# Two softmaxes of a decoder layer: sums taken before the turn, weights turned after the exponentials

## What is computed

```python
# self attention, 16 heads of 8
scores = einsum('bhid,bhjd->bhij', Q, K) / sqrt(8) + einsum('bhid,ijd->bhij', Q, rel_table[rel_idx])
ctx = einsum('bhij,bhjd->bhid', softmax(scores), V);  out = ctx @ Wo + bo
# cross attention, 16 heads of 64, keys and values from the 77 context tokens
sim = einsum('bihd,bjhd->bhij', x @ Wq, context @ Wk) * 64**-0.5
out = einsum('bhij,bjhd->bihd', softmax(sim), context @ Wv) @ Wo
```

## Time and profile before

| | |
|---|---|
| runs | 845.19, 846.94, 856.15 us; median 846.94 |
| profiled execution | 846.87 us, its span 845.1 us |
| busy, share of the span | TensorE 718.3 us (85%), VectorE 518.2 (61%), ScalarE 417.1 (49%), GpSimd 205.9 (24%) |
| mean granted TensorE clock | 0.938 of full speed |

### The profile page before, as it was taken

How to read it: one execution, slowest core, us unless ns; L and a number is a source line. 1 busy time by engine, 2 the same in 40 slices (tenths; PEclk the granted TensorE clock), 3 DMA queues, 4 the chain that set the end, 5 groups by cost and what they waited for, 6 DMA issues and landing times. The chain is left out here.

```text
span 845.1 us, 22574 instructions
## 1 busy us (share of the span) xinstructions
PE 718.3 (85%) x9462; PEld 538.8 (64%) x9462; DVE 518.2 (61%) x1447; ACT 417.1 (49%) x1188; POOL 205.9 (24%) x212
## 2 busy tenths in 40 slices
PE   5788998999998798999874887898888888988873
PEld 3466776677776576776664685666666666766641
DVE  1343665555557655655565575777878877788732
ACT  3745656456556355566432122345555554555531
POOL 5210011111101110115314022334333334333200
PEclk9989999999999799999998796999999999999975
DMA  9534444233444214444422110000000000110000
GB/s 361 206 123 129 153 154 154 104 126 93 141 154 154 107 48 154 153 151 153 144 90 101 50 41 17 8 11 15 14 12 11 12 11 13 15 16 11 5 5 6
DMA packets 48261, 72.30 MB, mean 86 GB/s; under 512 B 2832, under 2 KB 43280, under 8 KB 45472
## 3 DMA queue, kind: packets, MB, share of 16 engines
q1 hardware_dynamic: 45120, 61.80, 21.5%
q0 software_dynamic: 2320, 5.18, 2.8%
q10 hardware_dynamic: 720, 3.88, 1.2%
HBM read 32.38 MB, written 38.47 MB: 84 GB/s over the span
## 5 line engine op out<-in xcount | busy, mean ns | idle before, releaser
L403 POOL TENSOR_TENSOR rext<-rext,ones 128x1008 f32<-128x1008 f32 x16 | 29.9, 1867 | 320.5 <-ACT rext L919 320.5
L934 ACT ACTIVATE sc<-sc,nmxa 128x128 f32<-128x128 f32 x256 | 78.2, 388 | 7.0 <-DVE nmxa L1149 6.3
L972 ACT ACTIVATE pTb<-bank 77x512 f32<-77x512 f32 x128 | 66.8, 590 | 7.3 <-PE bank L486 7.3
L1199 DVE TENSOR_REDUCE nmb<-bank 128x4 f32<-128x308 f32 x128 | 53.7, 472 | 16.6 <-PE bank L486 16.5
L1438 DVE TENSOR_TENSOR k<-bank,k_sb 128x512 f32<-128x512 f32 x64 | 41.2, 685 | 35.5 <-PE bank L486 35.5
L1145 DVE TENSOR_TENSOR sc<-bank,rel 128x512 f32<-128x512 f32 x64 | 41.1, 684 | 21.3 <-PE bank L486 21.3
L464 POOL TENSOR_SCALAR k<-k 128x256 f32<-128x256 f32 x16 | 13.8, 860 | 160.2 <-ACT k L1048 160.2
L486 PE MATMUL bank<-k,xdT 128*128 128x512 f32 x96 | 49.3, 654 | 0.0
L919 ACT ACTIVATE rext<-bank 128x512 f32<-128x512 f32 x64 | 35.6, 592 | 27.0 <-PE bank L486 27.0
L534 PE MATMUL bank<-k_sb,sc 128*128 128x128 f32 x256 | 42.3, 289 | 7.0 <-ACT sc L934 4.7
L486 PE MATMUL bank<-nmT,k_sb 32*77 32x128 f32 x1024 | 47.6, 280 | 0.0
(11 more groups left out here) (267 smaller groups left out, 1744.5 us busy)
## 6 DMA issues: line engine op xcount, KB each, us to landing
rel_dram<-rext SPq DMA_DIRECT2D x16, 2040.0 KB
rel<-rel_dram SPq DMA_DIRECT2D x16, 960.0 KB, 5.5
rext<-w_up SPq DMA_DIRECT2D x1, 1792.0 KB, 10.7
rel<-w_down SPq DMA_DIRECT2D x1, 1792.0 KB, 7.7
wb<-w_b ACTq DMA_DIRECT2D x1, 1604.0 KB, 16.5
xT_ld<-xT SPq DMA_DIRECT2D x16, 64.0 KB, 6.8
x_all<-x ACTq DMA_DIRECT2D x1, 1024.0 KB, 11.7
rel<-rel_dram SPq DMA_DIRECT2D x16, 64.0 KB, 5.8
```

What stands on the lines that cost most here:

```text
L403: G.tensor_tensor(rext[:, :, 0:MAX_REL - 1], rext[:, :, MAX_REL - 1:MAX_REL].broadcast_to(shape), ones[:, 0:1].unsqueeze(2).broadcast_to(s ...
L934: last = A.activation(sc[:, h, :], sc[:, h, :], ACT.Exp, bias=nmxa[:, h:h + 1])
L972: A.activation(dst[0:C, 4 * i:4 * i + 4, :], bank[b][0:C, :].rearrange("p (a i) -> p a i", a=4), ACT.Exp).then_inc(exped["b"], 1)
L1199: V.tensor_reduce(nmb[:, 32 * i:32 * i + 4], bank[b][:, 0:4 * C].rearrange("p (a j) -> p a j", a=4), AX.X, ALU.max, negate=True).then_inc( ...
```

## The change

The cross attention's scores stay with the queries on the partitions. VectorE subtracts the maxima while it copies them from the banks to `pB` in SBUF (`b_l0` to `b_l3`), ScalarE takes the exponentials there, four of 128x308; the banks are free from `b_l` on, and `v0`, `b_v`, `b_r` and others use them meanwhile. VectorE sums 8 heads at a time (`b_sum0`, `b_sum1`) and takes reciprocals (`b_rec0`, `b_rec1`), GpSimd multiplies `pB` by them (`b_n0`, `b_n1`, 128x616 each), TensorE turns the 16 heads by transposes (`b_t0` to `b_t3`), and ScalarE and VectorE copy two banks each to `pTb`. `b_u0`, `b_u1` become plain copies. `b_nm`, `b_st0`, `b_st1`, `b_inj`, `b_sm0`, `b_sm1` and `b_rc` are gone.

In the self attention each of the 16 exponentials also writes the sum of its row (`accum_out`). VectorE takes the reciprocals (`a_rec`), widens them to 128x128 (`a_rw`), TensorE transposes this (`a_rT`) and ScalarE copies it to `rba`; the sums by matmul and the Ln and Exp are gone.

`ORDER1` is new for all engines but SP, with a deeper pipeline: `a_s` of a sequence is in round t, `b_t` and `b_out` in t+3, the logits in t+4, the slots in t+5. `r_send` handles one sequence a round instead of a batch. `pB` lies over the key weights, `x1` has three buffers, and some semaphores of loop 2 are replaced by others that exist already.

```diff
 ORDER1 = {
-    "pe": ("b_inj:-1 a_t2 a_t3 a_qkv:2 a_v b_sm0:-1 b_sm1:-1 b_v0:-1 b_v1:-1 rel_last:2 a_out b_out:-1 rel:2 "
-            "v0 b_r:-1 b_x b_lg:-1 r_rank:-2 a_s:1 b_q b_s0 b_s1 a_t0:1 b_st0 b_nm a_t1:1 b_st1").split(),
+    "pe": ("b_t0:-3 b_t1:-3 b_t2:-3 b_t3:-3 a_s b_q:-2 b_s0:-2 a_v:-1 a_qkv:2 b_s1:-2 a_rT:-1 b_v0:-3 b_v1:-3 "
+            "a_out:-1 b_r:-4 b_out:-3 rel_last:2 b_lg:-4 v0:-2 r_rank:-5 rel:2 b_x:-1 a_t0 a_t1 a_t2 a_t3").split(),
+    "dve": ("b_norm:-4 b_t1:-3 b_t3:-3 a_m0 a_m1 b_qhi:-2 b_m0:-2 b_m1:-2 b_l0:-2 b_m2:-2 b_l1:-2 b_l2:-2 "
+            "b_m3:-2 a_div:-1 b_l3:-2 b_u0:-3 b_u1:-3 a_qkv:2 a_add:-1 b_sum0:-2 a_st:-1 rel_last:2 a_ag:-1 "
+            "b_sum1:-2 b_rec0:-2 b_add:-3 b_lg:-4 a_ln:-1 r_a:-4 a_rec b_rec1:-2 b_st:-3 r_b:-4 a_rw r_c:-5 "
+            "b_ag:-3 a_t1 v0:-2 a_t3").split(),
+    "act": ("a_t0:-1 b_ln:-4 a_t2:-1 b_t0:-3 b_t2:-3 b_qlo:-2 a_e0 a_e1 a_qkv:2 a_rT:-1 b_e0:-2 b_e1:-2 a_e2 "
+            "b_e2:-2 b_r:-4 b_e3:-2 a_e3 a_ln:-1 r_a:-4 v0:-2 rel0:2 rel1:2 rel2:2 rel3:2 b_x:-1").split(),
+    "pool": "r_send:-12 rel_fill:2 b_n0:-1 b_n1:-1".split(),
...
+        early = sb("early", [P, H * C])
+        wk = early[:, 0:WK_N]
+        pB = early[:, :].rearrange("p (h j) -> p h j", j=C)
...
+        x1 = [sb(f"x1{i}", [P, P]) for i in range(3)]
...
+            def b_even_(j):
+                def f(t):
+                    pool.wait_ge(recips["b"], 2 * t + 1 + j)
+                    part = slice(8 * j, 8 * j + 8)
+                    G.tensor_tensor(pB[:, part, :], pB[:, part, :], recb[:, part].unsqueeze(2).broadcast_to([P, 8, C]),
+                                    ALU.mult).then_inc(b_even, 1)
...
             def send(t):
+                pool.wait_ge(r_slots, 2 * sum(1 for b in BATCHES if b[0] <= t) - 1)
...
             def a_scores(t):
                 pe.wait_ge(a_kv, t + 1)
-                need(pe, var["a"], t)
+                need(pe, a_pT_act, 2 * t)
+                need(pe, a_pT_dve, 2 * t)
...
             def a_turn(i):
                 def f(t):
                     pe.wait_ge(exped["a"], 4 * t + i + 1)
+                    if t + 2 < B:
+                        pe.wait_ge(r_mid, 4 * (t + 2) + i + 1)
...
+            def a_rT_(t):
+                pe.wait_ge(recips["a"], t + 1)
...
+                pe.transpose(bank[1][:, P:2 * P], recw[:], ident).then_inc(a_rT_ps, 1)
...
+            def b_turn(i):
+                def f(t):
+                    pe.wait_ge(b_even, 2 * t + 1 + i // 2)
...
+                    for a in range(4):
+                        last = pe.transpose(bank[(6, 7, 4, 5)[i]][0:C, a * P:(a + 1) * P], pB[:, 4 * i + a, :], ident)
+                    last.then_inc(turned, 1)
...
             def b_values(j):
                 def f(t):
-                    pe.wait_ge(exped["b"], 4 * t + 2 + 2 * j)
+                    pe.wait_ge(b_pT_act, 2 * t + 1 + j)
+                    pe.wait_ge(b_pT_dve, 2 * t + 1 + j)
+                    if t + 1 < B:
+                        pe.wait_ge(maxed["b"], 4 * (t + 1) + 1 + 2 * j)
...
             def a_exp(i):
...
-                        last = A.activation(sc[:, h, :], sc[:, h, :], ACT.Exp, bias=nmxa[:, h:h + 1])
+                        last = A.activation(sc[:, h, :], sc[:, h, :], ACT.Exp, bias=nmxa[:, h:h + 1],
+                                            accum_out=suma[:, h:h + 1])
...
+            def b_exp(i):
+                def f(t):
+                    act.wait_ge(maxed["b"], 4 * t + i + 1)
+                    part = pB[:, 4 * i:4 * i + 4, :]
+                    A.activation(part, part, ACT.Exp).then_inc(exped["b"], 1)
...
+            def a_wide(t):
+                past("a_rec", t)
+                need(dve, a_rT_ps, t)
+                V.tensor_copy(recw[:].rearrange("p (h d) -> p h d", d=DH), reca[:].unsqueeze(2).broadcast_to([P, H, DH])
+                              ).then_inc(recips["a"], 1)
...
+            def a_div(t):
+                dve.wait_ge(a_rT, t + 1)
+                dve.wait_ge(values["a"], t + 1)
+                V.tensor_tensor(oTa[:], bank[0][:, 0:P], rba[:], ALU.mult).then_inc(oT_ready["a"], 1)
...
+            def b_less(i):
+                def f(t):
+                    past(f"b_m{i}", t)
+                    need(dve, turned, 4 * (t - 1) + i + 1)
+                    V.tensor_tensor(pB[:, 4 * i:4 * i + 4, :], bank[(6, 7, 4, 5)[i]][:, 0:4 * C].rearrange(
+                        "p (a j) -> p a j", a=4), nmxb[:, 4 * i:4 * i + 4].unsqueeze(2).broadcast_to([P, 4, C]), ALU.add
+                        ).then_inc(maxed["b"], 1)
...
+            def b_sum(j):
+                def f(t):
+                    dve.wait_ge(exped["b"], 4 * t + 2 + 2 * j)
+                    keep(f"b_sum{j}", t, V.tensor_reduce(sumb[:, 8 * j:8 * j + 8], pB[:, 8 * j:8 * j + 8, :], AX.X, ALU.add))
```

More of the change, by code:

```diff
@@ L700, in _ @@
                 "a_qkv": a_qkv_, "rel": rel_scores, "rel_last": rel_last,
-                "a_s": a_scores, **{f"a_t{i}": a_turn(i) for i in range(4)}, "a_v": a_values, "a_out": a_out,
-                "b_x": b_x, "b_q": b_q_, "b_s0": b_scores(0), "b_s1": b_scores(1), "b_nm": b_nm, "b_st0": b_turn(0),
-                "b_st1": b_turn(1), "b_inj": b_inj, "b_sm0": b_sums_(0), "b_sm1": b_sums_(1),
+                "a_s": a_scores, **{f"a_t{i}": a_turn(i) for i in range(4)}, "a_v": a_values, "a_rT": a_rT_, "a_out": a_out,
+                "b_x": b_x, "b_q": b_q_, "b_s0": b_scores(0), "b_s1": b_scores(1), **{f"b_t{i}": b_turn(i) for i in range(4)},
                 "b_v0": b_values(0), "b_v1": b_values(1), "b_out": b_out,
@@ L1212, in b_mul, with b_out, f @@
+            def b_out(j):
+                def f(t):
+                    dve.wait_ge(values["b"], 2 * t + j + 1)
+                    V.tensor_copy(oTb[:, 4 * j:4 * j + 4, :], bank[4 if j else 6][:].rearrange(
+                        "p (c i) -> p c i", c=4)).then_inc(oT_ready["b"], 1)
                 return f
@@ L1327, in _ @@
                 "a_qkv": a_kv_, "rel_last": rel_last, "a_m0": a_max(0), "a_m1": a_max(1), "a_t1": a_turn(1),
-                "a_t3": a_turn(3), "a_div": divide("a", 0, rba[:], oTa[:]),
-                "a_add": add("a", 1, lambda t: x_all[:, t, :]), "a_st": stats_("a"), "a_ag": moments("a"), "a_ln": norm("a", lambda t: x1[t % 2][:], normed["a"]),
-                "b_qhi": b_qhi_, **{f"b_m{i}": row_max(i, (6, 7, 4, 5)[i]) for i in range(4)},
-                "b_u0": b_mul(0), "b_u1": b_mul(1), "b_add": add("b", 7, lambda t: x1[t % 2][:]),
+                "a_t3": a_turn(3), "a_rec": a_recips, "a_rw": a_wide, "a_div": a_div,
+                "a_add": add("a", 1, lambda t: x_all[:, t, :]), "a_st": stats_("a"), "a_ag": moments("a"), "a_ln": a_norm,
+                "b_qhi": b_qhi_, **{f"b_m{i}": b_max(i) for i in range(4)},
+                **{f"b_l{i}": b_less(i) for i in range(4)},
+                "b_t1": b_turn(1), "b_t3": b_turn(3), "b_sum0": b_sum(0), "b_sum1": b_sum(1), "b_rec0": b_recips(0), "b_rec1": b_recips(1),
+                "b_u0": b_out(0), "b_u1": b_out(1), "b_add": add("b", 7, lambda t: x1[t % 3][:]),
                 "b_st": stats_("b"), "b_ag": moments("b"),
```

216 lines of the change are left out of this document (122 added, 94 removed).

## The result

The changed kernel takes 823.83 us (median of 819.17 to 825.33) against 847.16 for before: ratio of the means 0.9695, 95% interval 0.9616 to 0.9774. The forecast was 823. The time is right, but not all of its steps are: the steady round came out 2 us shorter than was forecast, and the start and the routing batches cost most of that back.

What follows compares the result with a forecast made beforehand. It took TensorE's own instructions to bound loop 1's round before. A walked round of 21.75 plus 0.3 and 0.45 gave 22.5; loop 1 ending at 446 against 469.9 saved 24 us: 845.1 - 24 + 1.8 = 823, range 806 to 850.

Steps and rivals of the forecast that it cites:

- The forecast's own case: Loop 1's steady round becomes 22.0 to 23.1 us, the time 817 to 832; chance 0.45.
- rival A: Accumulators and GpSimd holds both cost nothing in loop 1: round 21.3 to 21.8, time 806 to 814; chance 0.15.
- The path: Loop 1's new round walked from b_t0 over VectorE, TensorE and ScalarE in turn: 21.75 us before two additions.
- The charge of 0.3 for accumulators: ScalarE's accumulator sums in the self attention delay the round by 0.3 us, at 0.2 us extra per exponential.
- x: Extra price of accum_out per ScalarE exponential in the self attention: taken as 0.2 us, bounds 0 to 0.305.
- The charge of 0.45 for holds: GpSimd's fill and b_n0 hold VectorE's b_norm and a_ln, adding 0.45 us a round.
- Batch 0, 8 us: Routing batch 0's VectorE chains in loop 1, pick 6 and slots 2.5, cost 8 us, against 11.4 before.
- Rounds 0 to 2: Loop 1's first rounds, chains without full cross attention, take 17, 14 and 16.5 us; round 3 starts at 81.5.
- TensorE's floor of 20.5: TensorE's work per round of loop 1 falls from 22.7 to 20.5 us, the floor of the new round.
- D: ScalarE becomes the bound at 0.5 us extra per exponential: round 25.5 or more, time 862 and up; chance 0.11.
- C: Round gains nothing, VectorE held longer or accumulators dearer: round 23.2 to 24.5, time 833 to 850; chance 0.29.
- TensorE's own instructions set the round: In loop 1 of before, TensorE is busy 22.7 of the steady round's 23.86 us and so bounds it.

Runs made afterwards that it cites:

- e7: The changed kernel with each b_sum done twice on VectorE, the first result unused; 826.7 us, steady round 20.91.
- e8: The changed kernel with one more unused 128x512 reduction in a_m1 on VectorE, ahead of b_qhi; 848.7 us, round 23.93 in the trace.
- e11: e8 with the 32 unused matmul records of the self attention's sums added on TensorE behind a_v; 833.6 us, round 21.27.
- e3: The changed kernel without accum_out on the self attention's 16 exponentials, row sums a constant 8; 823.0 us, round 20.55.
- e1: The changed kernel with rel_fill ahead of the two sends in GpSimd's queue; 821.2 us, round 20.55.
- e6: e1 with VectorE's two normalisations, b_norm and a_ln, moved out of GpSimd's instructions; 821.2 us, round 20.81.
- e5: The kernel before with only the self attention's half of the change; 845.7 us against 849.9 for before, round 24.12.
- e9: e6 with the pick of a batch moved on VectorE one round later, behind b_u1; 807.3 us, ratio 0.9481 to before.
- e13: The changed kernel with the self attention's half undone, the cross attention's half and the new order kept; 821.4 us, ratio 0.9659.
- e10: e1 with the pick of a batch moved behind b_u1 as in e9, normalisations where the changed kernel has them; 810.7 us.

## Why the prediction was right, step by step

Where its sum stood against the trace, in us:

| step | predicted | measured | difference |
|---|---|---|---|
| round 3 starts | 81.5 | 87.2 | +5.7 |
| nine steady rounds, 3 to 11 | 202.5 | 185.3 | -17.2 |
| rounds 12 to 15 | 95.0 | 102.9 | +7.9 |
| rounds 16 and 17 | 31.0 | 29.9 | -1.1 |
| round 18 to the slots of batch 1 | 15.7 | 19.7 | +4.0 |
| 16 sends | 20.3 | 19.9 | -0.4 |
| last send ends | 446 | 444.9 | -1 |

So the sum is right to 1 us out of terms wrong by up to 17. The direction and the range rest on a mechanism that held; that the time came out at 823 is luck, errors that cancelled. The forecast's own case asked for a round of 22.0 to 23.1, and 20.55 lies below even rival A's 21.3.

- **The path: right, and shown** (e7, e8, e11). The walk's stations from b_t0 of the steady round, predicted and seen: b_t3 3.45 and 2.7, b_qhi 8.95 and 8.5, last b_l 12.8 and 12.0, b_u1 14.1 and 13.1, b_out 15.4 and 14.5, v0 17.9 and 16.7, end 21.75 and 20.55. In order, none missing, 1.2 us long in all. Two thirds of that is one term: a transpose was sized at 0.165 from eight in two groups of four; sixteen in a row take 0.12 each, which is 0.8 at b_t alone.
- **The charge of 0.3 for accumulators: wrong** (e3). x is 0.08, not 0.2, and ScalarE covers it. That the bound from the nearest row (0.20 for a 128x1 instruction) was the record's length (0.19 is what the trace shows for the read) and not its distance to the next is the flaw: here the read overlaps the exponentials on both sides of it.
- **The charge of 0.45 for holds: the mechanism right, the place wrong** (e1, e6). The holds are there, on a_ln even longer than sized, and free in the steady round, since VectorE waits behind them. The walk itself had VectorE waiting at a_t1, and the charge was added without asking that.
- **Batch 0, 8 us: sized far too low.** Rounds 12 and 13 exceed steady ones by 9.5 and 8.0, and 14 by 3.9. The sentence "hidden since the next store has a round's time", on the sends ahead of rel_fill, looked only at the store; the late fills held b_norm for 4.11 and 3.73, and e1 wins back 3.6 us of it. And the pick was taken at 6 us, without the fill that holds three of its steps, and without TensorE's low clock after the gap (0.89 and 0.82 in these rounds).
- **Rounds 0 to 2: 53.6 in place of 47.5.** The clock was taken as low once, in one round; it was low in all three (0.70, 0.62 and 0.81 on average), and the third round took 19.2 in place of 16.5.
- **TensorE's floor of 20.5** was not a floor: its busy time fell to 19.2, again by the transposes. VectorE's 19.2 was 18.4.
- **Rivals.** D, ScalarE the bound, is out with x = 0.08. C, no gain in the round, is out; a_rw, which it took as held by GpSimd, takes 0.20 in the steady round of after (at 228.06) and is not held. A was right that the two additions are nothing in the steady round, but its 21.3 to 21.8 was too long still.
- **"TensorE's own instructions set the round" of before: open** (e5). With 0.53 us less of them the round did not fall, but a_t3 then waited for ScalarE's longer exponentials; a kernel without that was not run.

## What to carry to other kernels

Walk the round engine by engine in the queues' order and mark where each waits: time added beside the path was seen at 14 to 26% here, time added on the path in full (0.72 of 0.72), and in an execution in which TensorE's clock fell behind the longer wait, at nearly five times (3.4 for 0.72). Take the price of an instruction from the distance to its neighbour in a row of its like, not from its record. When an instruction is put ahead of others in a queue, ask not only who needs those, but also whom they will block when they run late.

## What the runs showed of the hardware

- **The price of a short stretch at the lower clock.** With TensorE's wait before a_qkv at 0.30 (e11), 0.45 (after) and 0.71 us (e9) the steady rounds ran at a granted clock of 1.00; with it at 1.18 (e8, the execution of 856.1 us) 7.8 us of each round ran at 0.56. With matmuls that nobody needs in the wait (e11, another chip) the clock was 1.00 and the round 21.27 in place of 23.93. It is no fixed limit on that wait: e8's own runs spread from 837 to 856 us, and two rounds of e13 had such a stretch without it.
- **VectorE held by GpSimd** over two instructions in a row: 4.11 us for a normalisation of 0.34, from 0.3 us before the first fill began to the end of the second. Steps of the pick with two SBUF inputs were held as well, a multiplication of 128x64 for 0.79 and a comparison for 1.56, where both take 0.22 free.
- **Before on one chip takes 878.7 us**, 3.4% more than on the others, while the kernels derived from after took about as long there as elsewhere (e10 810.7 there, e9 807.3 on another). The mean granted clock of before is 0.908 to 0.918 there and 0.917 to 0.945 elsewhere; that is not all of it, since an execution at 0.917 takes 861.1 elsewhere and three at 0.918 take 872.9 to 878.7 there. No trace of before on that chip was taken; the reason is open.
